# x1's squares in 32-row tiles, and an odd slab's y of squares and fields in two halves of its columns

## The reference

```
x = x0
for k in (k1, k2, k3):
    x = einsum('bmd,bhd,mho->bod', x0, x, k.reshape(32, x.shape[1], -1))
    finals.append(sum(x, axis=-1))
logit = concatenate(finals, axis=-1) @ kf
```

## Time and profile before

| | |
|---|---|
| median of 3 runs | 305.47 us (304.95 to 306.73) |
| profiled execution, its own time | 306.67 us |
| profiled execution, first to last instruction (span) | 304.7 us |
| mean granted TensorE clock | 0.988 |
| busy: PE / ACT / POOL / DVE | 295.1 / 241.6 / 228.3 / 195.1 us |
| PE in contract / features / rotate | 229.1 / 31.4 / 26.4 us |

### The profile page before, as it was taken

One profiled execution on the slowest core, in us unless ns is written; L12 is line 12 of the kernel. 1 busy time (PEld: TensorE's weight loads), 2 busy tenths in 40 slices (PEclk: granted clock), 3 DMA queues, 4 the chain that ended last, 5 costly groups with the idle time before them and its releaser, 6 DMA issues.

```text
span 304.7 us, 7927 instructions
## 1 busy us (share of the span) xinstructions
PE 295.1 (97%) x3189; PEld 87.0 (29%) x3189; DVE 195.1 (64%) x211; ACT 241.6 (79%) x232; POOL 228.3 (75%) x132
## 2 busy tenths in 40 slices
PE   7769999999999999999999999999999999999996
PEld 2442222222322222222222222232222222222221
DVE  1635857657777666667766666677766666777632
ACT  1564997979979797988979797997979798897921
POOL 7456967878798687878788687879868787878800
PEclk9968999999999999999999999999999999999999
DMA  7999999594876849486784838487683839500000
GB/s 244 405 412 421 389 407 407 186 352 203 319 307 247 347 148 345 169 344 258 304 315 189 357 142 353 198 318 301 254 342 148 360 150 346 224 0 2 2 0 1
DMA packets 15414, 77.84 MB, mean 255 GB/s; under 512 B 1832, under 2 KB 2088, under 8 KB 7720
## 3 DMA queue, kind: packets, MB, share of 16 engines
q1 hardware_dynamic: 15256, 77.49, 64.9%
q10 hardware_dynamic: 144, 0.15, 0.3%
HBM read 77.63 MB, written 0.01 MB: 255 GB/s over the span
## 4 chain that ended last, share of the span: by engine, by line
PE 94%; DMA 2%; issue 1%; DVE 1%; ACT 1%; SPq 0%; DVEq 0%
PE acc L558 74%; PE acc L566 10%; PE rot L544 8%; DMA xc<-x_chunks 2%; PE acc L590 1%; PE acc L577 1%; ACT prod L198 1%; PE acc L637 0%; SPq L236 0%; DVE xy L492 0%; DVE sums L495 0%; DVE low L456 0%; ACT split L303 0%; PE acc L631 0%; PE acc L614 0%
## 5 line engine op out<-in xcount | busy, mean ns | idle before, releaser
L558 PE MATMUL acc<-prod,w 128*32 128x512 f32 x2048 | 229.1, 598 | 0.2 <-issue 0.2
L389 POOL TENSOR_TENSOR prod<-u,v 128x1024 f32<-128x1024 f32 x64 | 152.9, 2390 | 14.9 <-PE acc L558 11.1
L558 PEld LDWEIGHTS acc<-prod,w 128*32 128x32 f32 x2048 | 64.1, 110 | 147.7 <-issue 133.7
L283 ACT ACTIVATE prod<-rot 128x1024 f32<-128x1024 f32 x64 | 65.3, 1021 | 25.4 <-PE rot L544 24.9
L485 DVE TENSOR_TENSOR prod<-rot,u 128x1024 f32<-128x1024 f32 x64 | 77.7, 1214 | 4.8 <-PE rot L544 4.8
L492 DVE SCALAR_TENSOR_TENSOR xy<-acc,kzs,xsb 128x512 f32<-128x512 f32 x32 | 24.0, 751 | 85.8 <-ACT xsb L312 80.0
L485 DVE TENSOR_TENSOR prod<-rot,v 128x1024 f32<-128x1024 f32 x64 | 77.6, 1213 | 0.0
L399 POOL TENSOR_TENSOR split<-low,split 128x512 bf16<-128x512 f32 x31 | 36.1, 1165 | 32.1 <-ACT split L307 32.1
L291 ACT COPY feat<-u 32x2048 f32<-32x2048 f32 x31 | 58.9, 1899 | 0.6
L287 ACT ACTIVATE feat<-u 96x2048 f32<-96x2048 f32 x31 | 58.8, 1898 | 0.0
L395 POOL TENSOR_TENSOR low<-xc,split 128x512 f32<-128x512 f32 x31 | 36.2, 1167 | 10.1 <-ACT split L303 9.9
(11 more groups left out here) (44 smaller groups left out, 29.6 us busy)
## 6 DMA issues: line engine op xcount, KB each, us to landing
u<-u_rows SPq DMA_DIRECT2D x30, 1024.0 KB, 4.8
v<-v_rows SPq DMA_DIRECT2D x30, 1024.0 KB, 6.9
xc<-x_chunks SPq DMA_DIRECT2D x32, 256.0 KB, 6.9
u<-u_rows SPq DMA_DIRECT2D x4, 512.0 KB, 9.7
v<-v_rows SPq DMA_DIRECT2D x4, 512.0 KB, 11.7
u<-k3p SPq DMA_DIRECT2D x2, 512.0 KB, 5.3
v<-k2t SPq DMA_DIRECT2D x1, 512.0 KB, 6.7
fixs<-fixes SPq DMA_DIRECT2D x1, 256.0 KB, 7.6
```

The lines of the kernel that those rows point to most:

```text
L283: nc.scalar.activation(prod[p][:, WW, pair(n)], rot[:, pair(n)], ACT.Square).then_inc(squares_ready, 1)
L389: nc.gpsimd.tensor_tensor(prod[p][:, UV, pair(half)], us[n][:, pair(half)], vs[n][:, pair(half)], ALU.mult).then_inc(uv_ready, 2)
L558: mm = nc.tensor.matmul(acc[p][h][quad(c), :], w[:, t, h * G:(h + 1) * G], prod[p][:, t, chunk(c)], start=(t == first), stop=(first is Non ...
```

## The change

It touches how the `feat` part reaches the accumulators.

- **x1**: the weights `wf` for x1 are taken as 32 rows, not 64. For an even slab in the steady state they are read from quad 1 (`feature(p, 0, wf, quad(1), ...)`), for the odd one that is opened from quad 0. (Slabs 0 and 1 take `quad(0)`, and close as before with y's 64 rows.) No zero rows are needed, so the memset of `wf` goes.
- **y of an odd slab**: its columns are taken in two halves of each chunk (`part(0)`, `part(1)`, 256 columns each). For half 0 the squares and fields stand in the upper rows 64 to 127, as before; for half 1 they stand in the lower rows 0 to 63, with a second copy `wy` of the weights. ACT therefore writes an odd slab's `feat` in four instructions of 4x256 columns in place of two of 2048 (`square_odd_fields`, `copy_odd_fields`).
- **the order on PE**: at the end of an even step `features_of_two` issues the even slab's y (upper rows, 512 columns), the odd slab's y of half 1 (lower rows, 256 columns), the even slab's x1 (quad 1), the odd slab's x1 (quad 0). The odd slab's y of half 0 (upper rows, 256 columns) follows after the next `rotate`, ahead of the odd slab's `contract`. A new semaphore `half_opened` is waited for ahead of that `rotate`.
- **the set-up**: four more small 32-column matmuls in `fold`, and one more DVE copy (`wy`).

```diff
-        fold_ps = [acc[1][0][0:M, 2 * G:3 * G], acc[1][1][2 * M:3 * M, 2 * G:3 * G]]
-        rest_ps = acc[1][1][2 * M:, 2 * G:3 * G]
+        fold_ps = acc[1][0][0:2 * M, 2 * G:3 * G]
+        rest_ps = acc[1][1][:, 2 * G:3 * G]
...
+            def square_odd_fields(s, p, n):
+                act.wait_ge(acc_ready, s - 1)
+                for half, rows in enumerate((FEATS, quad(0))):
+                    nc.scalar.activation(by_chunk(feat[p])[rows, :, part(half)], by_chunk(us[n])[rows, :, part(half)],
+                                         ACT.Square)
+
+            def copy_odd_fields(p, n):
+                for half, q in enumerate((3, 1)):
+                    copy = nc.scalar.copy(by_chunk(feat[p])[quad(q), :, part(half)], by_chunk(us[n])[quad(q), :, part(half)])
+                copy.then_inc(feat_ready, 1)
...
-                    square_fields(s + 1, q, m)
-                    if n % 2 == 0:
-                        copy_fields(q, m)
+                    if n % 2:
+                        square_fields(s + 1, q, m)
+                    else:
+                        square_odd_fields(s + 1, q, m)
+                        copy_odd_fields(q, m)
...
-            nc.vector.memset(wf[:], 0.0).then_inc(wf_cleared, 1)
...
+            nc.vector.tensor_copy(wy[:], rest_ps[0:2 * M, :]).then_inc(wy_ready, 1)
...
-            def features(p, opens=False):
-                for h, rows in enumerate((slice(0, 2 * M), slice(2 * M, 4 * M))):
-                    for c in range(CHUNKS):
-                        mm = nc.tensor.matmul(acc[p][h][quad(c), :], wf[rows, :], feat[p][rows, chunk(c)], start=opens,
-                                              stop=not opens, skip_group_check=True)
...
+            def feature(p, h, weights, rows, opens, closes, columns=slice(0, CHUNK)):
+                for c in range(CHUNKS):
+                    mm = nc.tensor.matmul(acc[p][h][quad(c), columns], weights[rows, :],
+                                          by_chunk(feat[p])[rows, c, columns], start=opens, stop=closes,
+                                          skip_group_check=True)
+                return mm
+
+            def features(p):
+
+                feature(p, 0, wf, quad(0), False, True).then_inc(x1_ready, 1)
+                feature(p, 1, wf, UPPER, False, True).then_inc(acc_ready, 1)
+
+            def features_of_two(p):
+
+
+                feature(p, 1, wf, UPPER, False, True)
+                feature(1 - p, 1, wy, LOWER, True, False, part(1)).then_inc(half_opened, 1)
+                feature(p, 0, wf, quad(1), False, True).then_inc(x1_ready, 1)
+                feature(1 - p, 0, wf, quad(0), True, False).then_inc(acc_ready, 1)
...
+                    if n % 2 and (not isinstance(s, int) or s > 1):
+                        pe.wait_ge(half_opened, 2 * it + n // 2)
                     rotate((n + 1) % 2)
+
+                if n % 2 and (not isinstance(s, int) or s > 1):
+                    if isinstance(s, int) and s + 1 == SLABS:
+                        pe.wait_ge(half_opened, SLABS // 2 - 1)
+                    feature(p, 1, wf, UPPER, False, False, part(0))
...
-                features(p)
-                features(1 - p, opens=True)
+                features_of_two(p)
```

More of the change, by code:

```diff
@@ L37 @@
 SECOND = {UW: (ZERO, C), VW: (A, B_)}
+LOWER, UPPER = slice(0, 2 * M), slice(2 * M, P)
 HALFWAY = slice((Q - 1) * M, P)
@@ L132, in cin_kernel @@
         wf = sb("wf", [P, G])
+        wy = sb("wy", [2 * M, G])
         kf1 = kzs[:, KF1]
@@ L157, in cin_kernel @@
         idle_ready, ones_ready = sem("idle_ready"), sem("ones_ready")
-        tt_cleared, wf_cleared = sem("tt_cleared"), sem("wf_cleared")
+        tt_cleared = sem("tt_cleared")
         vt_ready, vts_ready, v_done, v_ready = (sem(n) for n in ("vt_ready", "vts_ready", "v_done", "v_ready"))
@@ L163, in cin_kernel @@
         fold_ready = [sem(f"fold_ready{h}") for h in range(2)]
-        wf_ready = [sem(f"wf_ready{h}") for h in range(2)]
+        wf_ready, wy_ready = [sem(f"wf_ready{h}") for h in range(2)], sem("wy_ready")
         picks_ready = sem("picks_ready")
@@ L175, in cin_kernel @@
         first_feat = sem("first_feat")
+        half_opened = sem("half_opened")
         taken = sem("taken")
@@ L209, in pair, with part, by_chunk @@
             return slice(n * PAIR, (n + 1) * PAIR)
+        def part(half):
+            return slice(half * CHUNK // 2, (half + 1) * CHUNK // 2)
+        def by_chunk(x):
+            return x[:].rearrange("p (c n) -> p c n", n=CHUNK)
         def chunk(c):
@@ L504, in _ @@
             multiply_w(0, 0, 0, (0,))
-            dve.wait_ge(wf_cleared, 1)
             dve.wait_ge(fold_ready[0], 1)
-            nc.vector.tensor_tensor(wf[quad(0), :], k1s[quad(0), 2 * TILES, :], fold_ps[0], ALU.add
+            nc.vector.tensor_tensor(wf[0:2 * M, :], k1s[0:2 * M, 2 * TILES, :], fold_ps, ALU.add
                                     ).then_inc(wf_ready[0], 1)
             dve.wait_ge(fold_ready[1], 1)
-            nc.vector.tensor_copy(wf[2 * M:, :], rest_ps).then_inc(wf_ready[1], 1)
+            nc.vector.tensor_copy(wf[2 * M:, :], rest_ps[2 * M:, :]).then_inc(wf_ready[1], 1)
+            nc.vector.tensor_copy(wy[:], rest_ps[0:2 * M, :]).then_inc(wy_ready, 1)
             def step(it, n):
@@ L596, in fold @@
                 pe.wait_ge(fixed, 2)
-                mm = nc.tensor.matmul(fold_ps[h], kzs[:, FOLD], w[:, WW, h * G:(h + 1) * G], start=True,
-                                      stop=(h == 0), skip_group_check=True)
+                for q in (0, 1) if h == 0 else (0, 2):
+                    mm = nc.tensor.matmul((fold_ps if h == 0 else rest_ps)[quad(q), :], kzs[:, FOLD],
+                                          w[:, WW, h * G:(h + 1) * G], start=True, stop=(h == 0), skip_group_check=True)
                 if h == 1:
[L600 to L603, removed]
+                    for q in (0, 2):
+                        nc.tensor.matmul(rest_ps[quad(q), :], diagonal((ZERO, ZERO), 0, 0), kzs[:, 2 * M:3 * M],
+                                         start=False, stop=True, skip_group_check=True)
+                    for q in (1, 3):
+                        mm = nc.tensor.matmul(rest_ps[quad(q), :], t_places[:, M:2 * M, WRAP], kzs[:, 2 * M:3 * M],
+                                              start=True, stop=True, skip_group_check=True)
                 mm.then_inc(fold_ready[h], 1)
@@ L664, in _ @@
                 pe.wait_ge(wf_ready[h], 1)
+            pe.wait_ge(wy_ready, 1)
             features(0)
```

## The result

The changed kernel takes 317.15 us (median of 3 runs, 316.08 to 318.71) where the kernel before takes 305.47: 1.039 times as long, 95% interval 1.033 to 1.045. Run again beside the later kernels it gave 318.64 us against 306.21, ratio 1.040 (1.035 to 1.045). That is 11.7 to 12.4 us more; the forecast was 16.2 more, 321.7 us, within 314 to 325.

What follows compares the result with a forecast made beforehand. PE was taken to bind, meeting an equally long chain through ACT and POOL at rotate in even steps. Terms 8.3 + 0.1 + 5.9 + 1.8 + 0.1 = 16.2 us on 305.47 gave 321.7 us, range 314 to 325.

Steps and rivals of the forecast that it cites:

- ACT's loop: Chain from rotate through ACT and POOL to the next rotate; claimed as long as PE's own chain in the even step.
- the forecast's own case: Whole kernel: tile shapes drain and the chain through ACT and POOL binds at rotate; 319.5 to 324 us, chance 0.40.
- the two rivals at 317.5: Whole kernel: tile shapes overlap while ACT's chain binds (0.24), or shapes drain while that chain doesn't bind (0.16); 317.5 us each.
- the ACT term: Even step: ACT's four feature instructions take 4.25 us against 3.83, so POOL's last part and split_ready come 0.42 us later.
- y's half behind rotate: Odd step, between rotate and contract: 0.43 us of matmuls plus a 0.12 change of shape, unhidden; 15 x 0.55 = 8.3 us.
- rotate late after an even step: At rotate: 0.42 later from ACT, less 0.1 slack, plus 0.1 for a register instruction; 14 x 0.42 = 5.9 us.
- last pair: End of the last even step, where no rotate follows: the change of shape between y and x1 costs 0.1 us.
- slabs 0 and 1: Start of the kernel: x1 in 32 rows and y in 64 add 0.98 us each, 0.18 hidden at slab 0; 1.8 us.
- the rest: Set-up: four small matmuls beside others and a DVE copy of 64x32, 0.1 us; dropped memset and later x1 cost nothing.
- Shapes run side by side: PE: different tile shapes overlap, ACT's chain binds; the half costs about 0.40, slabs 0 and 1 nothing; 317.5 us, chance 0.24.
- Shapes drain, ACT's loop doesn't bind: At rotate: short ACT instructions overlap or slack is near 0.37, so rotate comes only 0.12 later; 317.5 us, chance 0.16.
- Faster: PE: shapes overlap and rotate's upper tiles start before x1 ends, needing split_ready by 101.5; -6 us, 299.5 us, chance 0.05.

Runs made afterwards that it cites:

- single-shape run: Changed kernel with both x1 groups at the end of an even step in 64 rows instead of 32, so all four groups share one shape: 321.21 us, ratio 1.053.
- ACT's part alone: Kernel before with only the odd slab's squares and fields on ACT split into four instructions of 4x256 columns, PE untouched: 305.16 us, ratio 0.999.

## Why the prediction was right, and what was off

The direction was right, and so was the picture of PE: the half of y lies bare, and x1 waits for y. The part on ACT's loop was not. The sum was 16.2 us and the measurement says about 12, so the forecast's own case (0.40, with 319.5 to 324) did not happen; the range of 314 to 325 holds the result because the lower bounds of its terms and the two rivals at 317.5 had been taken in. Of the signs that the forecast named, the stretch between rotate and contract is there (0.57 for 0.55), and x1 starts 0.99 after y (for 0.98). ACT's four instructions took 4.12 us and not 4.25, the pair 18.16 and not 18.4. The idle time of some 0.3 us ahead of rotate, released by POOL's last part, is missing (PE is busy for all of a pair), and by the forecast's own words that makes the ACT term wrong. The time alone couldn't have shown it: the rival in which nothing drains and ACT's loop binds had 317.5 as well. By its own terms:

| term | forecast | found | from |
|---|---|---|---|
| y's half behind rotate | 15 x 0.55 = 8.3 | 15 x 0.57 = 8.5 | timeline; the run without it |
| rotate late after an even step | 14 x 0.42 = 5.9 | 14 x 0.19 = 2.7 | pair 18.16 - 17.40 less 0.57; 0.14 is the change of shape, 0.05 ACT's loop |
| last pair | 0.1 | 0.1 | timeline |
| slabs 0 and 1 | 1.8 | 0.7 + 1.0 - 0.45 (slab 2) = 1.2 | timeline |
| the rest | 0.1 | not seen | |
| sum | 16.2 | 12.5 | times: 11.7 to 12.4; at the same clock 12.2 to 12.3 |

**Shapes.** "Bounds: nothing, or the second shape waits for all of the first. I take the second." That held: x1 in 32 rows starts 0.99 after y, where 0.45 would do, and with one shape it does start then. The Trainium skill's sentence in "TensorEngine Tiling (Array Packing)", section "Tiling Modes", that changing the tiling mode drains TensorE, covers tiles that don't overlap as well; the 0.13 to 0.14 us per change are of these runs.

**The half.** Right in size and in that nothing hides it.

**ACT's loop.** The step that was mis-sized, and it makes up most of the difference. Two of its numbers were off, both the same way. The four instructions cost 0.29 us, not 0.42, since neighbouring squares overlap by about 0.1; the forecast had this as its lower bound. The slack was 0.2 us and not 0.1; I had read 0.3 us of queue waits as if all of it stood between the last part and rotate, and the copy on ACT shows that rotate needs 0.22. And I compared the delay with PE's own chain as if only the larger of them counted (0.42 against 0.12), which was right, but after the correction the loop exceeds PE's 0.14 by 0.05 only. The extra register instruction costs its 0.1 (0.33 after the last part against 0.22): 0.29 + 0.1 - 0.2 = 0.19, and 0.19 - 0.14 = 0.05 is what the run with ACT as before gave back.

**Slabs 0 and 1.** They cost 0.72 and 0.96, 1.7 together; the forecast had 1.8. But at slab 2 the kernel before had a wait that the changed one, coming later, doesn't have, which the forecast overlooked and which gave 0.45 back. PE of the kernel before at slab 2:

```profile
40.92 6.21 PE L558 MATMUL acc<-prod,w 128*32 128x512 f32 x56
47.38 1.06 PE L558 MATMUL acc<-prod,w 128*32 128x512 f32 x8 [0.24 <-issue]
```

Its last tile starts 6.46 after the first, 0.45 later than in a contract of 7.07 us, whose last 1.06 us begin at 6.01; in the changed kernel no such gap shows (39.75, 7.07 for all 64). This is read from the two timelines; no run was made for it.

**The rivals.** "Shapes run side by side" is refuted by x1's start at 0.99 in the changed kernel, with the single-shape run beside it. "Shapes drain, ACT's loop doesn't bind" was the nearest, 317.5 by its sum and 317.15 measured: the loop binds by 0.05 us. "Faster" needed both doors open and both were shut. The other rule that the forecast weighed stands in the Trainium skill, page "TensorE: Matmul & The Clock Gate", section "The mechanism" of its Part 3: matmuls keep program order in their starts and in their ends. Beside rows 11, where a later matmul starts ahead of an earlier one, the runs disagree on the ends too. With one shape the second passes of `wy` start at 101.97; the second passes of the group issued before them start at 102.16. With 0.215 us for 256 columns and 0.43 for 512, the first end at about 102.19 and the others at about 102.59 (an estimate from these rows). The first passes of the two groups start in order, 101.71 and 101.73.

The changed kernel uses three quarters of the cells for a pair's features (64 x 512 + 64 x 256 + 2 x 32 x 512 + 64 x 256 rows times columns for a chunk, against 4 x 64 x 512), and takes longer, because what it saves are cells in tiles that ran beside others anyway (x1's rows of zeros), and what it adds is time in sequence: 0.43 us of matmuls and two changes of shape in each pair. No kernel of these runs beats the one before; the groups of one shape, all eight side by side, are the best arrangement of those tried.

## What to carry to other kernels

Count TensorE's work in passes that follow each other, not in cells used: in these runs smaller tiles could only have gained beside other tiles of the same shape, and every change of shape cost a wait for all that was in flight. When an engine at 97% gets company, measure the slack of the loop behind it with a copy of known length before pricing a change by it; here ACT's loop cost 0.7 us in all, and without the 0.2 us of slack it would have been 14 x 0.25 = 3.5 (an estimate from the terms above). And look for the wait that a delay removes elsewhere, as at slab 2.

## What the runs showed of the hardware that I had not expected

- A change between tiles of 64 and of 32 rows that have no row in common holds the second until the first is through: 0.99 us where 0.45 would do. A group of 0.43 us in the upper rows, moved to where the lower rows were free, was paid in full as well (its PSUM bank was also x1's).
- Within one shape the second pass of a later matmul starts ahead of the second pass of an earlier one whose tile is still busy: 101.97 ahead of 102.16 in the single-shape kernel.
- A register instruction more in PE's queue ahead of a matmul shows as about 0.1 us: rotate followed POOL's last part by 0.33 us in the changed kernel (0.32 to 0.38 over the loop) and by 0.22 in the one with the extra copy on ACT (0.22 to 0.24), both times as the one that was waited for.
- ACT's pieces of 4x256 columns cost no more than straight runs of 1024: 1042 and 1045 ns against 1046 and 1043. Two copies in a row took 1.99 us where both wrote the same rows (ACT's part alone) and 2.11 where they wrote rows 96 to 127 and then 32 to 63 (the changed kernel); why was not tested.
